# Deformable-convolution samplers: products of hats on one engine, one wide copy of four banks, wider final products, full-width turns

## The reference, cut to what matters

```python
off = conv2d(x, w_off, b_off)                      # 18 planes: dy, dx of 9 taps
ys = base_y + ky*2 + dy;  xs = base_x + kx*2 + dx  # where each tap looks
sampled = bilinear(x, ys, xs)                      # 4 neighbours, weights (1-fy)(1-fx) ...
out = einsum('oik,bikhw->bohw', w_dc, sampled)     # 9 taps x 64 channels -> 64
x1 = relu(bn(out))            # first;  second: relu(bn(out) + x)
```

## Time and profile before

| | |
|---|---|
| median of three runs | 762.95 us |
| lowest, highest | 751.47, 770.78 us |
| span of the profiled execution | 772.1 us |
| TensorE products busy | 648.3 us, 84% |
| VectorE busy | 466.2 us, 60% |
| ScalarE busy | 369.2 us, 48% |
| GpSimd busy | 292.6 us, 38% |
| mean granted TensorE clock | 0.857 of full |

### The profile page before, as it was taken

How to read it: one execution, slowest core, us unless ns; L and a number is a source line. 1 busy time by engine, 2 the same in 40 slices (tenths; PEclk the granted TensorE clock), 3 DMA queues, 4 the chain that set the end, 5 groups by cost and what they waited for, 6 DMA issues and landing times.

```text
span 772.1 us, 32568 instructions
## 1 busy us (share of the span) xinstructions
PE 648.3 (84%) x14954; PEld 478.2 (62%) x14954; DVE 466.2 (60%) x560; ACT 369.2 (48%) x568; POOL 292.6 (38%) x287
## 2 busy tenths in 40 slices
PE   6579888888884899889986477999999999995566
PEld 1156666666721667666665466888888888873344
DVE  0588768766406877776852716366766666666433
ACT  0265556545314555555451233466655565563521
POOL 4054566464200555455541142334344434320300
PEclk9858999988987589998789755799999999997758
DMA  8310000000004000000001530000000000000002
GB/s 294 83 20 4 4 4 5 4 3 3 5 5 93 3 4 4 4 4 3 5 3 29 112 116 1 2 1 0 0 0 0 0 0 0 0 2 1 0 2 110
DMA packets 6407, 18.06 MB, mean 23 GB/s; under 512 B 1869, under 2 KB 4237, under 8 KB 5573
## 3 DMA queue, kind: packets, MB, share of 16 engines
q1 hardware_dynamic: 6286, 16.24, 7.5%
HBM read 12.37 MB, written 3.87 MB: 21 GB/s over the span
## 4 chain that ended last, share of the span: by engine, by line
PE 74%; DVE 8%; issue 6%; ACT 5%; DMA 4%; POOL 1%; SPq 1%; DVEq 0%; POOLq 0%; ACTq 0%
PE banks L268 21%; PE banks L199 10%; PE banks L844 9%; PE banks L888 5%; PE banks L821 5%; PE banks L869 5%; PE banks L903 4%; PE banks L171 3%; PE banks L185 2%; ACT y L301 2%; DMA off<-in_places_dram 2%; PE banks L834 1%; PE banks L229 1%; PE banks L615 1%; DMA off<-offsets_dram 1%
## 5 line engine op out<-in xcount | busy, mean ns | idle before, releaser
L322 POOL TENSOR_TENSOR y<-hy,hx 128x576 f32<-128x576 f32 (+1 forms) x104 | 167.5, 1632 | 212.8 <-DVE hy L396 206.9
L268 PE MATMUL banks<-y,xt 32*64 32x144 f32 (+1 forms) x6656 | 169.3, 309 | 26.9 <-issue 15.9
L268 PEld LDWEIGHTS banks<-y,xt 32*64 32x64 f32 x6656 | 115.3, 147 | 57.3 <-issue 38.0
L322 DVE TENSOR_TENSOR y<-hy,hx 128x576 f32<-128x576 f32 (+1 forms) x104 | 121.8, 1215 | 5.0 <-DVE hy L396 0.5
L1085 POOL TENSOR_TENSOR y<-y,stats 128x1024 f32<-128x1024 f32 x32 | 60.8, 1900 | 109.2 <-DVE stats L1017 109.1
L349 ACT ACTIVATE hx<-banks 128x768 f32<-128x768 f32 x96 | 62.1, 651 | 62.2 <-PE banks L171 61.1
L301 DVE COPY y<-banks 128x768 f32<-128x768 f32 x48 | 45.8, 955 | 76.0 <-PE banks L268 76.0
L354 ACT ACTIVATE hy<-banks 128x768 f32<-128x768 f32 (+1 forms) x92 | 71.7, 805 | 40.1 <-PE banks L185 39.6
L199 PE MATMUL banks<-y,w_dc 64*64 64x128 f32 x2304 | 84.3, 299 | 4.0 <-issue 2.8
L1007 DVE TENSOR_REDUCE stats<-banks 128x16 f32<-128x1024 f32 x32 | 39.2, 1225 | 72.8 <-PE banks L844 72.8
L199 PEld LDWEIGHTS banks<-y,w_dc 64*64 64x64 f32 x2304 | 74.6, 150 | 11.5 <-issue 9.4
(11 more groups left out here) (141 smaller groups left out, 828.1 us busy)
## 6 DMA issues: line engine op xcount, KB each, us to landing
src<-in_x_dram SPq DMA_DIRECT2D x4, 578.0 KB, 5.7
y<-in_w_dram SPq DMA_DIRECT2D x1, 2080.0 KB
xt<-in_xt_dram SPq DMA_DIRECT2D x1, 2048.0 KB, 11.5
off<-in_w_dram SPq DMA_DIRECT2D x2, 1024.0 KB
out_dram<-tokens SPq DMA_DIRECT2D x4, 512.0 KB, 2.7
offsets_dram<-tokens SPq DMA_DIRECT2D x32, 54.0 KB
off<-offsets_dram SPq DMA_DIRECT2D x16, 108.0 KB
w_dc<-in_w_dc_dram SPq DMA_DIRECT2D x2, 288.0 KB, 9.0
```

What stands on the lines that cost most here:

```text
L268: last = nc.tensor.matmul(ap(out, [[UNIT_ROWS * PITCH - 2, 3], [PITCH, strip.n], [1, WIN_COLS]]), m.xt[32 * j:32 * j + 32, strip.tile_row, ...
L322: multiply(dst, hy, hx, ALU.mult).then_inc(cv.s_ready[g], 1)
```

## The change

1. `weigh` runs on VectorE alone: two products per strip (`g` = 0, 1) and one semaphore. GpSimd keeps only the copies for the turn, in the first convolution.
2. `take` is one ScalarE copy of all four banks, 128x1536 elements; VectorE copies none.
3. `final_pe` multiplies two image pairs at once (256 columns) and comes once per row, behind the unit with `ky` = 0; `finish0` and `finish1` handle all four pairs.
4. `columns_pe` makes all three `kx` of two tile columns in one product each of 144 columns, 4 per item, where there were 8 of 96 and 8 of 48.
5. `turn_pe` makes 4 transposes of 128x128 in place of 16 products of 32 output rows, and comes one row earlier.
6. In the items `y` now comes before `x`; behind the units with `ky` = 1 and 2 stand the two `x` items, inside them the `y` items.

```diff
-        self.coords = [("x", u, 0), ("x", u, 1)] + [("y", u, k) for k in range(len(self.y_items))]
+        self.coords = [("y", u, k) for k in range(len(self.y_items))] + [("x", u, 0), ("x", u, 1)]
...
-            final = [("f", row - 1, ky)] if row and ky < 2 else []
-            turn = [("t", row - 2)] if turns and row >= 2 and ky == 2 else []
-            cut = len(todo) if final else (len(todo) + 1) // 2
+            final = [("f", row - 1)] if row and ky == 0 else []
+            turn = [("t", row - 1)] if turns and row and ky == 2 else []
+            cut = len(todo) if final else len(todo) - 2
             unit.inside, unit.behind = todo[:cut], todo[cut:] + final + turn
...
-    kx, n = (0, 2) if part == 0 else (2, 1)
-    for c in range(TC):
+    for c in (2 * part, 2 * part + 1):
         for g in range(2):
             rows = group_rows(g, 1)
...
     for tap in range(TAPS):
-        for p in (k, k + 2):
+        for q in range(2):
             for g in range(2):
...
-                last = nc.tensor.matmul(m.ps[C * g:C * g + C, bank + p // 2, 0:PLACES], cv.w_dc[rows, tap, :],
-                                        m.sampled[rows, row % 2, p, tap, :], start=(tap == 0),
+                last = nc.tensor.matmul(pair_sums(m, bank, q)[C * g:C * g + C, :, :], cv.w_dc[rows, tap, :],
+                                        m.sampled[rows, row % 2, 2 * q:2 * q + 2, tap, :], start=(tap == 0),
...
     for c in range(TC):
-        for j in range(PAIRS):
-            last = nc.tensor.matmul(m.ps[32 * j:32 * j + 32, bank, c * P:(c + 1) * P], m.stage[:, tile_row % 2, j, c, :],
-                                    m.identity[:, :], start=True, stop=True, skip_group_check=True)
+        last = nc.tensor.transpose(m.ps[:, bank, c * P:(c + 1) * P],
+                                   m.stage[:, tile_row % 2, c, :, :].rearrange("p i n -> p (i n)"), m.identity[:, :])
...
-def take(copy, m, cv, unit, j):
-    return copy(ap(m.sampled[:, unit.row % 2, j, 3 * unit.ky, :], [[TAPS * PLACES, 2], [W, 3 * UNIT_ROWS], [1, W]]),
-                ap(m.ps[:, j, 4:], [[BANK, 2], [PITCH, 3 * UNIT_ROWS], [1, W]]))
+def take(copy, m, cv, unit):
+    return copy(ap(m.sampled[:, unit.row % 2, 0, 3 * unit.ky, :], [[TAPS * PLACES, PAIRS], [W, 3 * UNIT_ROWS], [1, W]]),
+                ap(m.ps[:, 0, 4:], [[BANK, PAIRS], [PITCH, 3 * UNIT_ROWS], [1, W]]))
...
-    multiply(dst, hy, hx, ALU.mult).then_inc(cv.s_ready[g], 1)
+    for g in range(2):
...
+        made = nc.vector.tensor_tensor(dst, hy, hx, ALU.mult)
+    made.then_inc(cv.s_ready, 1)
...
-        take_waits(dve, cv, unit)
-        take(nc.vector.tensor_copy, m, cv, unit, 2).then_inc(cv.taken[1], 1)
```

More of the change, by code:

```diff
@@ L140 @@
 PLANS = [Plan(True), Plan(False)]
[L141 removed]
+FINALS = len(UNITS) // 3
 class Conv:
@@ L241, in item_pe @@
         bank = ring_banks(n)
+        if item[0] in "xy" and item == cv.plan.units[3 * HALF_ROWS // UNIT_ROWS].coords[0]:
+            pe.wait_ge(cv.moved[1], MOVES)
         if item[0] == "x":
-            if item[1:] == (3 * HALF_ROWS // UNIT_ROWS, 0):
-                pe.wait_ge(cv.moved[1], MOVES)
             columns_pe(nc, m, cv, bank, item[1], item[2])
@@ L248, in item_pe @@
         elif item[0] == "f":
-            for taker in range(2):
-                pe.wait_ge(cv.taken[taker], 3 * (item[1] + 1))
-            if cv.k and item[1:] == (0, 0):
+            pe.wait_ge(cv.taken, 3 * (item[1] + 1))
+            if cv.k and item[1] == 0:
                 pe.wait_ge(m.w_scaled, 1)
-            final_pe(nc, m, cv, bank, item[1], item[2])
+            final_pe(nc, m, cv, bank, item[1])
         else:
@@ L284, in sampler_pe @@
         if unit.u:
-            for taker in range(2):
-                pe.wait_ge(cv.taken[taker], unit.u)
+            pe.wait_ge(cv.taken, unit.u)
         started = 0
@@ L334, in item_act @@
         if item[0] == "f":
-            if cv.k and item[1:] == (0, 0):
+            if cv.k and item[1] == 0:
                 act.wait_ge(cv.moved[1], MOVES)
-            cv.finish(item[1], item[2], bank).then_inc(cv.finished, 1)
+            cv.finish(item[1], bank).then_inc(cv.finished, 1)
             return
@@ L343, in item_act @@
         u = item[1]
-        if item[0:3] == ("x", u, 0) and u >= 2:
-            for g in range(2):
-                act.wait_ge(cv.s_ready[g], cv.plan.units[u - 1].before)
+        if item == cv.plan.units[u].coords[0] and u >= 2:
+            act.wait_ge(cv.s_ready, cv.plan.units[u - 1].before)
         if item[0] == "x":
-            first, end = (0, 2 * X_HATS // 3) if item[2] == 0 else (2 * X_HATS // 3, X_HATS)
-            nc.scalar.activation(m.hx[:, u % 2, :, first:end], m.ps[:, bank:bank + 2, 0:end - first], ACT.Abs
+            nc.scalar.activation(ap(m.hx[:, u % 2, 0, 2 * item[2] * X_TILE:], [[X_HATS, 2], [TC * X_TILE, 3], [1, 2 * X_TILE]]),
+                                 ap(m.ps[:, bank, :], [[BANK, 2], [2 * X_TILE, 3], [1, 2 * X_TILE]]), ACT.Abs
                                  ).then_inc(cv.emptied, 1)
@@ L372, in sampler_pool @@
 def sampler_pool(nc, pool, m, cv):
-    def stage(tile_row):
-        pool.wait_ge(cv.finished, 2 * tile_row + 2)
+    for tile_row in range(TR):
+        pool.wait_ge(cv.finished, tile_row + 1)
         if tile_row >= 2:
@@ L377, in stage @@
         stage_pool(nc, m, tile_row)
[L379 to L386, removed]
 def sampler_dve(nc, dve, m, cv):
     def hats(unit):
-        dve.wait_ge(cv.emptied, cv.plan.count[unit.coords[1]])
+        dve.wait_ge(cv.emptied, cv.plan.count[unit.last_y])
+        hat = m.hy[:, unit.u % 2, :, 0:unit.hat_rows * HAT_ROW]
+        nc.vector.tensor_scalar(hat, hat, 1.0, 1.0, ALU.min, ALU.subtract).then_inc(cv.hats, 1)
+        dve.wait_ge(cv.emptied, cv.plan.count[unit.last_x])
         hat = m.hx[:, unit.u % 2, :, :]
-        nc.vector.tensor_scalar(hat, hat, 1.0, 1.0, ALU.min, ALU.subtract).then_inc(cv.hats, 1)
-        dve.wait_ge(cv.emptied, cv.plan.count[unit.coords[-1]])
-        hat = m.hy[:, unit.u % 2, :, 0:unit.hat_rows * HAT_ROW]
         nc.vector.tensor_scalar(hat, hat, 1.0, 1.0, ALU.min, ALU.subtract).then_inc(cv.hats, 1)
```

103 lines of the change are left out of this document (56 added, 47 removed).

## The result

Four executions of the changed kernel took 782.19 us (median; 778.59 to 784.89); the kernel before took 761.96 us beside them. The ratio is 1.033, with a 95% interval of 1.023 to 1.043; it leaves out executions that the comparison counts as disturbed, so it isn't quite the quotient of the medians. The forecast of "no change", 764 us, failed; the time lies inside its range of 738 to 788, where the second rival (the clock falls at the new waits, 787 us) had put it. The third rival (VectorE becomes the bound) had 780 us, nearer still, but its sign, TensorE waiting for line 332, is absent: 1.5 us in all.

What follows compares the result with a forecast made beforehand. TensorE's work and waits were taken to set the time. Sampler terms summed to about 0, plus 2 us for the clock: 774 us against the profiled 772.1, a median of 764 us, range 738 to 788.

Steps and rivals of the forecast that it cites:

- the second rival: Ends of units with ky = 1 and 2: the clock falls once more per row and convolution; 787 us, chance 0.20.
- The third rival: Samplers: VectorE becomes the bound if its products of hats stay at 1.28 and 1.02 us; 780 us, chance 0.04.
- The step that failed: Clock in both samplers: idle time per row as large as before, waits one unit apart; +2 us taken.
- Term 5: Steady row: 104 to 124 fewer weight loads shorten stops for instruction supply; 0.7 us saved, bounds nothing to 1.5.
- stops still every 127 weight loads: Sign of being right: TensorE's stops for instruction supply keep their spacing of 127 weight loads, shorter in sum.
- The totals: Rows and ends summed: second sampler +1.6 us, first -1.4, together about 0.
- the first rival: Samplers: instruction supply is the bound, so all stops and most half-clock stretches vanish; 729 us, chance 0.26.
- Terms 1 to 4 and 6 to 8: Finals, take, items, turn (+0.9 us a row second convolution, +0.6 first); then VectorE's hat products, ScalarE's load, ends.
- term 4: Turn, first convolution: wait for take and one item's emptying +0.47 us, transposes -0.38, together +0.1 a row.
- term 1: Final products: one of twice the columns takes 3.9 us in place of 1.95; alone saves only 0.2 us a row.

Runs made afterwards that it cites:

- the filling: The changed kernel with four products of zeros in each TensorE wait for the copy behind a unit: 728.31 us, ratio 0.956.
- With the clock held: The changed kernel with products of zeros in those waits and also ahead of each sampler's first item and first seven items: 723.27 us, ratio 0.950.
- the narrow finals: The changed kernel with the old 128-column final products, two a row behind ky = 0 and 1: 768.99 us, ratio 1.005.

## Why the prediction was wrong

The range held and the forecast in it did not. The sign that I had named for the second rival, a clock clearly under 0.85 in both samplers, is what came.

**The step that failed** is the clock: "idle time per row is as large as before [...] I take +2 us". The first half was not quite true. TensorE's waits for `take` and for items over both samplers rose by 27 us, while the stops for the supply of instructions fell by 18; all idle time rose from 40 to 48 us. The second half failed: the time at the lower clock rose by 88 us. At 0.385 us each that is 34 us, against the 2 that I took. I had priced every wait by its length, and left the clock as a small remainder.

**Term 5, fewer instructions** (0.7 us a row), was mis-sized too. The stops of the sampling, finals and items came to 21 us in both samplers before and to 3.4 after: 1.3 us a row, near the upper bound of 1.5. The sum: +34 from the clock, +27 from the waits and -18 from the stops are 43 us, and 18.6 were measured. So some 24 us of other work must have gone from TensorE's path, the items that now lie in waits and the finals and products that are fewer; that is what is left over and was not measured by itself. Of my signs of being right, "stops still every 127 weight loads" failed: 170 loads pass without one. The totals had a slip besides: the first sampler's took 0.8 us a row for this term where I had set 0.7, and counted its ends as 0.0 where those named come to +0.2; that is about 1 us.

**Rivals 1 and 2 were each true in part.** I had set them up as exclusive. The first had the stops vanish and "most half-clock stretches with them"; the stops nearly vanished, but the slow stretches grew, and went only with the filling. With the clock held, the kernel after takes 723 us (the first rival's 729); its second sampler has five finals between 268.79 and 342.94, 18.5 us a row, which is what that rival gave. With the clock not held it takes 782 (the second rival's 787). That its number came within 5 us is luck, for its parts were off and cancelled: it had 14 more falls at 1.7 us, and there were 6 more, each worth about 3.9 us (180 us x 0.385 over 18 stretches), and the older ones got longer.

**Terms 1 to 4 and 6 to 8 held where a row shows them.** `take` at 1.44 us; the boundary at 1.6 us for 1.7; the products at 752 and 452 ns; the start 0.6 us earlier for 0.5; VectorE at 103 and 100 us for 109, ScalarE at 104 and 99 for 105. The wait for a turn was 1.5 to 1.8 us for 1.2 before, near the +0.47 of term 4; its four loads took 0.42 us at the higher clock for 0.43. The final at the full clock took 3.66 us of weight loads for my 3.9, just below the 3.7 that I had named as the sign of an error in term 1; it is 0.24 us a row. In the filled kernel, first sampler:

```profile
105.40 3.66 PEld L198 LDWEIGHTS banks<-y,w_dc 64*64 64x64 f32 x72
105.40 4.12 PE L198 MATMUL banks<-y,w_dc 64*64 64x256 f32 x72
```

**What stays open.** Why the clock falls after one wait and not after another like it, and so how often it will. After the wait of 1.15 us at 340 us above it fell; after this one in the first sampler it stayed high for more than 10 us:

```profile
216.15 1.11 PE L279 MATMUL banks<-y,xt 32*64 32x144 f32 x53 [1.53 <-ACT y L311]
```

Why the narrow finals brought back so little of it is open too. What I read as chance in the attention was not tried either.

## What to carry to other kernels

Price a wait on TensorE by what the clock may do after it, not by its length: here 27 us more of waits, which shortened other work by nearly as much, went with 34 us of clock, and that hid a saving of 18. When a change leaves TensorE waiting at a fixed place, put products of zeros there, into a bank that is about to be overwritten, and see whether the clock and the time come back before judging the change. And ask of two rivals whether they exclude each other; a saving and a loss that are both real give a third time.

## What the hardware showed

With waits of mostly 1.0 to 1.5 us (the longest for `take` 1.6, for a turn 1.8), two or three in a row of tiles of 22 us, the granted clock was 0.76 and 0.74 in place of 0.88 and 0.85, and the kernel took 54 of 782 us more than with the waits filled, 7%. Stops of 0.8 to 1.4 us for the supply of instructions, too, had falls of the clock right behind them. The Trainium skill ("TensorE: Matmul & The Clock Gate", What's actually happening) puts the penalty of the ramp, the slow start of a run of products, at under 1% of a typical kernel's span. Falls in the middle are another matter, and here they cost more than that. The Trainium skill has them on the same page (A second HAM failure mode: psum-queue depth-cycling), where frequent short idle times between groups of products make the clock swing; these traces agree, with 16 falls in 358 us.

VectorE's product of two SBUF tiles took 752 ns without GpSimd at work and 1276 with it, 452 against 1020 for the shorter one. The Trainium skill ("SBUF — State Buffer", Who interferes with whom) states that such an instruction contends with GpSimd's reads; the traces agree. Moving GpSimd's half to VectorE therefore cost VectorE hardly anything: in the second sampler its products went from 61.6 to 64.4 us for twice the work.
